# The edge-attribute load of a fused two-layer graph kernel in nine pieces, spread over the item

## The reference

```python
h = relu(layernorm(x));  x = x + attention_layer(h, src, dst)      # 4 heads of 32
h = relu(layernorm(x));  x = x + edge_layer(h, src, dst, edge_attr_128)

# attention_layer
e = leaky_relu(a_s[src] + a_d[dst]);  m = segment_max(e, dst);  e = exp(e - m[dst])
out = segment_sum(e / segment_sum(e, dst)[dst] * xp[src], dst) + bias;  return relu(out)

# edge_layer
edge_agg = segment_sum(edge_attr @ We + be, dst)
x_comb = concat([x, edge_agg]);  h = x_comb + segment_sum(x_comb[src], dst)
return relu(h @ W1 + b1) @ W2 + b2
```

## Time and profile before

| | |
|---|---|
| median of 3 runs | 4222.09 us (4209.79 to 4226.62) |
| profiled execution | 4203.44 us |
| its span | 4200.3 us |
| PE busy | 2634.0 us (63%) |
| DVE busy | 1797.7 us (43%) |
| POOL busy | 1652.3 us (39%) |
| ACT busy | 1001.7 us (24%) |
| DMA, mean over the span | 150 GB/s |

### The profile page before, as it was taken

How to read it: one execution, slowest core, us unless ns; L and a number is a source line. 1 busy time by engine, 2 the same in 40 slices (tenths; PEclk the granted TensorE clock), 3 DMA queues, 4 the chain that set the end, 5 groups by cost and what they waited for, 6 DMA issues and landing times.

```text
span 4200.3 us, 62157 instructions
## 1 busy us (share of the span) xinstructions
PE 2634.0 (63%) x16749; PEld 2099.8 (50%) x16749; DVE 1797.7 (43%) x6117; ACT 1001.7 (24%) x2335; POOL 1652.3 (39%) x1625
## 2 busy tenths in 40 slices
PE   3455555555555555565555555555555559999999
PEld 2343444444444444444344444444444448888887
DVE  6444454445454444444445444444444541111111
ACT  2223223222222222222222222232222230000000
POOL 4544544454444444544455444544454410000000
PEclk7667676667666676666777776667666779999999
DMA  9444444444443444444444444444444446666665
GB/s 183 113 133 123 141 145 143 126 127 143 145 138 116 141 136 130 133 142 137 124 137 145 144 136 124 140 140 136 123 141 144 135 157 221 215 213 221 215 213 180
DMA packets 309819, 630.10 MB, mean 150 GB/s; under 512 B 115675, under 2 KB 239191, under 8 KB 276133
## 3 DMA queue, kind: packets, MB, share of 16 engines
q1 hardware_dynamic: 259679, 514.22, 36.1%
q0 software_dynamic: 50112, 115.56, 13.2%
HBM read 446.35 MB, written 183.24 MB: 150 GB/s over the span
## 4 chain that ended last, share of the span: by engine, by line
PE 42%; another core or an unknown queue 23%; issue 16%; DVE 9%; ACT 5%; SPq 3%; DMA 1%; DVEq 0%; ACTq 0%
PE pv L1184 11%; PE pv L1122 10%; PE pv L1056 8%; PE pt L1184 5%; ACT xsb L809 5%; PE pt L1066 3%; DVE big L1667 2%; PE pa L1066 1%; DVE lks L1650 1%; DVE tabb L1400 1%; PE pa L1110 1%; PE pm L1098 1%; DVE lin L1654 1%; DVE lin L1659 0%
## 5 line engine op out<-in xcount | busy, mean ns | idle before, releaser
L776 POOL DMA_INDIRECT big<-table,idx x1566 | 1615.6, 1032 | 1698.4 <-PE pv L1122 1220.0
L809 ACT ACTIVATE xsb<-pt 128x343 bf16<-128x343 f32 x1044 | 531.5, 543 | 1987.3 <-PE pt L1066 1029.0
L1066 PE MATMUL pt<-tabb 128*128 128x343 bf16 x1044 | 395.4, 381 | 819.9 <-ACT xsb L809 461.6
L1066 PEld LDWEIGHTS pt<-tabb 128*128 128x128 bf16 x1044 | 105.4, 101 | 1053.4 <-ACT xsb L809 577.5
L1056 PE MATMUL pv<-big 128*128 128x128 f32 x3132 | 629.4, 386 | 0.0
L1056 PEld LDWEIGHTS pv<-big 128*128 128x128 f32 x3132 | 613.0, 299 | 1.5
L1122 PE MATMUL pv<-big 128*128 128x133 f32 x3132 | 498.6, 326 | 162.3 <-DVE big L1667 162.3
L1122 PEld LDWEIGHTS pv<-big 128*128 128x128 f32 x3132 | 470.9, 234 | 182.9 <-DVE big L1667 175.5
L1184 PE MATMUL pv<-big,xsb 128*126 128x384 bf16 x2842 | 493.8, 327 | 19.0 <-DVE big L1695 19.0
L1184 PEld LDWEIGHTS pv<-big,xsb 128*126 128x126 bf16 x2842 | 382.8, 136 | 88.2 <-issue 19.0
L1400 DVE TENSOR_TENSOR tabb<-iotah,keyp 128x2064 bf16<-128x2064 bf16 x261 | 320.3, 1227 | 1.4 <-issue 1.1
(11 more groups left out here) (271 smaller groups left out, 2584.0 us busy)
## 6 DMA issues: line engine op xcount, KB each, us to landing
adj<-xsb SPq DMA_DIRECT2D x87, 1543.5 KB
big<-in_edge_attr_dram SPq DMA_DIRECT2D x87, 1152.0 KB, 5.2
xsb<-adj SPq DMA_DIRECT2D x58, 1543.5 KB, 6.7
selb<-rel SPq DMA_DIRECT2D x87, 576.0 KB
tabb<-adj SPq DMA_DIRECT2D x29, 1543.5 KB, 6.7
big<-table,idx POOLq DMA_INDIRECT x1566
state<-sums SPq DMA_DIRECT2D x87, 130.5 KB
sums<-state SPq DMA_DIRECT2D x87, 130.5 KB
```

Source lines behind the costliest of these rows:

```text
L776: pool.indirect_dma_start(out=V[b][:, j, 0:rows], out_offset=None, in_=table, in_offset=bass.IndirectOffsetOnAxis(ap=index[b][:, j:j + 1], ...
L809: return nc.scalar.activation(out_, in_, func, **kw).then_inc(s(name), 1)
L1066: nc.tensor.matmul(pab[c % 3], ohl[:, c, :], ohk[:, c, 0:KW], start=True, stop=True)\
```

## The change

The attributes are loaded in nine transfers of two j each (128 partitions by 256 float32) in place of one of 18 j. Item n of SP now loads those of item n+1, into the other buffer, not of item n+2. Piece 0 waits for `am_b` of item n-1, and pieces 1 to 8 wait for `g_step`, a semaphore that GpSimd raises ahead of every second gather: piece i goes out when gather 2i of item n+1 is about to be issued. Pieces 0 to 3 stand ahead of `store_peak`, pieces 4 to 8 behind the index load. The adjacency store stays one transfer (APIECES = 1), but its place in SP's order is now right behind piece 0.

```diff
-            def load_edges(n, b, it, start):
+            def load_index(b, it, start):
                 after_dma(sp, s(f"gat{b}"), it * J)
                 sp.sem_inc(s("sp_turn"), 1)
                 sp.dma_start(idx[b][:, :], src[bass.DynSlice(start, GE)].rearrange("(p j) -> p j", j=J))\
                     .then_inc(s(f"idx{b}"), 16)
-                after(sp, s("am_b"), n, 2)
-                sp.dma_start(AT[b], attr[bass.DynSlice(start, GE), :].rearrange("(p j) c -> p j c", j=J))\
+
+            def load_attr(b, start, i):
+                js = slice(i * PJ, (i + 1) * PJ)
+                sp.dma_start(AT[b][:, js, :], attr[bass.DynSlice(start, GE), :].rearrange("(p j) c -> p j c", j=J)[:, js, :])\
                     .then_inc(s(f"attr{b}"), 16)
...
+                def spread(lo, hi):
+
+                    for i in range(lo, hi):
+                        if not last:
+                            if i > 0:
+                                sp.wait_ge(s("g_step"), n * PIECES + (PIECES + i))
+                            elif not before_first:
+                                after(sp, s("am_b"), n, 1)
+                            load_attr(1 - b, following, i)
+                        if not before_first and i * APIECES % PIECES == 0:
+                            store_adjacency(n - 1, 1 - b, i * APIECES // PIECES)
+                spread(0, PIECES // 2)
                 store_peak(n, b, base)
-                if not isinstance(n, int) or n + 2 < NG - 1:
-                    load_edges(n + 2, b, it + 1, (n + 2) * GE)
-                elif n + 2 == NG - 1:
-                    load_edges(n + 2, b, it + 1, LAST)
+                if not isinstance(n, int) or n + 2 < NG:
+                    load_index(b, it + 1, LAST if isinstance(n, int) and n + 2 == NG - 1 else (n + 2) * GE)
+                spread(PIECES // 2, PIECES)
...
                 if not (isinstance(n, int) and n < 2):
                     store_projected(n - 2, base_of(n - 2))
-                if not before_first:
-                    store_adjacency(n - 1, 1 - b)
...
                 for j in range(J):
                     if n is not None and j % QUART == 0 and not (isinstance(n, int) and n < 2):
 
                         pool.wait_ge(s("vm_b"), n * QN + (j // QUART + 1 - 2 * QN))
-                        pool.sem_inc(s("g_started"), 1)
+                    if j % PJ == 0:
+                        pool.sem_inc(s("g_step"), 1)
...
-                pe.wait_ge(s(f"attr{b}"), it * 16 + 16)
+                pe.wait_ge(s(f"attr{b}"), (it * 16 + 16) * PIECES)
```

More of the change, by code:

```diff
@@ L57 @@
 FIN = 18
+PIECES = 9
+PJ = J // PIECES
+APIECES = 1
 MAGIC = 0x5f3759df
@@ L72 @@
 FARHI = 1 << 20
-assert COLS <= 128 and OFF <= 256 and NB * 128 <= NPAD and GE == J * 128
+assert J % PIECES == 0 and NB * COLS % APIECES == 0 and COLS <= 128 and OFF <= 256 and NB * 128 <= NPAD and GE == J * 128
 YCH = ((0, 13), (13, 25), (25, 37), (37, 49))
@@ L447, in _ @@
             for b in range(2):
-                load_edges(b, b, 0, b * GE)
+                load_index(b, 0, b * GE)
+            for i in range(PIECES):
+                load_attr(0, 0, i)
             for lo, hi in ((0, SPLIT), (SPLIT, NP)):
@@ L506, in store_projected, with store_adjacency @@
                 sp.dma_start(sums1[bass.DynSlice(base, WIN), :], fy[:, :]).then_inc(s("y_out"), 16)
[L508 to L510 removed]
+            def store_adjacency(n, b, i):
+                if i == 0:
+                    sp.wait_ge(s("ab_ev"), n * J + J)
+                cs = slice(i * (NB * COLS // APIECES), (i + 1) * (NB * COLS // APIECES))
+                sp.dma_start(adj[bass.DynSlice(n, 1), :, cs].rearrange("a p c -> (a p) c"), adjw[b].bitcast(BF16)[:, cs])\
                     .then_inc(s("adj_out"), 16)
@@ L533, in item @@
                     store_sums(n - 1, base_before)
+                last = isinstance(n, int) and n == NG - 1
+                following = 0 if last else LAST if isinstance(n, int) and n == NG - 2 else (n + 1) * GE
+                def spread(lo, hi):
[9 more added lines that the diff above has]
+                spread(0, PIECES // 2)
                 store_peak(n, b, base)
-                if not isinstance(n, int) or n + 2 < NG - 1:
-                    load_edges(n + 2, b, it + 1, (n + 2) * GE)
-                elif n + 2 == NG - 1:
-                    load_edges(n + 2, b, it + 1, LAST)
+                if not isinstance(n, int) or n + 2 < NG:
+                    load_index(b, it + 1, LAST if isinstance(n, int) and n + 2 == NG - 1 else (n + 2) * GE)
+                spread(PIECES // 2, PIECES)
                 if before_first:
@@ L560, in _ @@
             store_residual(NG - 1, base)
-            store_adjacency(NG - 1, 0)
+            for i in range(APIECES):
+                store_adjacency(NG - 1, 0, i)
             store_projected(NG - 1, base)
@@ L624, in extra_item @@
             def extra_item(n, b, it):
-                load_edges(n, b, it, extra(sp, 2, n, LAST))
+                start = extra(sp, 2, n, LAST)
+                load_index(b, it, start)
+                after(sp, s("am_b"), n, 2)
+                for i in range(PIECES):
+                    load_attr(b, start, i)
                 base = extra(sp, 1, n, N)
```

12 lines of the change are left out of this document (6 added, 6 removed).

## The result

The changed kernel took 4261.03 us (median of 4 runs, 4254.14 to 4273.44), the kernel before 4215.94 us (4 runs, three of them the ones that were known before the prediction): a ratio of 1.010, 95% interval 1.0065 to 1.0134. It was 45 us slower where no change was forecast. On which chip each of the two was timed is not on record, and from chip to chip the kernel before alone went from 4169 to 4197 us in later calls, so that part of this 1% can be the chip's.

What follows compares the result with a forecast made beforehand. The prediction took a per-item round of gather issue, late maxima and a chain to the next gathers, 38.1 us, to bound the first loop. Its terms summed to 0, leaving 4203 us profiled; forecast 4216 us, range 4070 to 4330.

Steps and rivals of the forecast that it cites:

- The sum over the ring: Total effect of the change on one item's round: 0 + 0 + 0 us, profiled execution staying at 4203 us.
- the ring: One item's round in the first loop: gather issue, late maxima, then weights and products releasing the next gathers; 38.1 us.
- the 2.5 us from the last gather to the maxima: Stretch after the last gather is issued until TensorE's late maxima are free for VectorE; 2.5 us, expected unchanged.
- the chain of 10 to 13 us: From the maxima through VectorE, TensorE and the weights to the products releasing the next gathers; 10 to 13 us.
- The slower rival: Moved transfers disturb TensorE's exchange of small results or slow gathers: 34 to 100 us, 560 if all items; chance 0.29.
- the one at 1411.96: Existing item with late exchange, 44.78 us, 6.7 over the mean; also cited for its first gather of 0.94 us.
- a longer way from the last gather to the maxima: Gathers landing later beside the store make the 2.5 us behind the last grow; 1 us each item is 84 us.
- the cover of pieces 4 to 8: Their issue on SP, 2.6 to 3.3 us, ends 1.5 us before the load of the sums, costing nothing.
- the first gather no faster: At the gathers' start, the first two stay at 1.5 and 1.3 us; a possible 80 us gain counted as nothing.
- the issue times of pieces 1 to 3: On SP behind the adjacency store, their gathers issued by +8.6 us; some 20 us of room, costing nothing.
- the DMA share of the first 9.65 us: DMA engines' share at the start of the gathers, 0.84 before, expected near 0.5 after the change.
- The rival "much faster": Other-queue traffic among the gathers makes TensorE's results prompt: 27 us an item, 924 us less, to 3300; chance 0.06.

Runs made afterwards that it cites:

- the first measurement: The changed kernel against the kernel before, 4 runs each, before any follow-up: medians 4261.03 and 4215.94 us, ratio 1.010; chips not on record.
- the first two calls: Follow-up sets, each on one chip: both kernels with the adjacency store moved or the attribute load cut, packed or placed differently; 1.0011 to 1.0523 of the kernel before.
- the store put back: The changed kernel with the adjacency store back at the item's end, nine pieces still spread: 1.0186 of the kernel before, later 1.0013 on a chip without late results.
- the cut by partitions: The changed kernel with its nine spread pieces cut into 15 partitions each instead of by j: 1.0157 of the kernel before, later 1.0032 on a chip without late results.
- six doubled products: Adjacency products of blocks 6 to 11 each made twice: in the changed kernel 0.9859, later 1.0002; in the kernel before 0.9851; all against the unmodified kernel before.
- a nudge: The kernel before with a tiny GpSimd memset ahead of gather 16 of every item, meant to delay the last two gathers: 1.0005 of the kernel before.

## Why the prediction was wrong, and where it was right

**The step that failed** is "The sum over the ring: 0 + 0 + 0 us an item. The profiled execution would stay at 4203 us." It prices what the change does to SP and the DMA queues and holds the two other parts of the ring, the 2.5 us from the last gather to the maxima and the chain of 10 to 13 us, as they were, without a reason. Neither stayed. In the mean the first grew by 0.51 us and the chain by 0.28, with 0.18 back from the gathers, 0.62 us an item. The chain is where it shows in the late items: it takes 10.3 us or 13 us according to whether the clock rises 3 us behind TensorE's restart or later, and restarts only 0.2 us apart lie on either side. In the first measurement 24 of 28 late items fell on the wrong side, where 5 of 21 had before. The rows to see it in were there: three items in a row of 37.06, 38.67 and 36.88 us, with a chain of 10.6 us in the first, where the text gives 10 to 13, and a PEclk of 0.82, 0.75 and 0.50 in the windows, that is, means over stretches at 1.2 and 2.4 GHz. I read them as a stable cycle and did not ask what kept it there.

**The slower rival** had the sign and half of the mechanism. It expected more items like the one at 1411.96; these went from 5 to 1. Its other half, a longer way from the last gather to the maxima, was there with 0.5 us where 1 us was priced, partly because the items in which the maxima came out early, as in the earlier trace rows, got fewer (7 with maxima before the last gather was issued, then 1). What it did not have is the clock.

**Right**: the cover of pieces 4 to 8 (2.65 us, ended before the load of the sums was due), no wait of TensorE for attributes, `am_b` no longer waited for, the first gather no faster (1.52 us before, 1.72 after, in the median), nothing from the signals of GpSimd. So the adjacency store, which no longer stands ahead of the gathers, wasn't what slowed them. That it is VectorE fits the trace of the kernel before: of the 238 gathers over 1.1 us 209 ran beside its writing of selection matrices (line 1400), of the 1328 others 81. The item at 1411.96 that the prediction leans on is one of these 81, for VectorE wrote such a matrix from 1412.00 on, beside its gather of 0.94 us; taken alone it would speak against VectorE as well. **Mis-sized**: the issue times of pieces 1 to 3, +7.7 to +10.7 us in the median where +8.6 at the latest was expected, later in single items; and the DMA share of the first 9.65 us, 0.65 for "near 0.5". No effect of either on the ring was seen.

**The rival "much faster"**, results that come promptly, exists as a state: 3388 us, close to the 3300 worked out. But what brings it is not this change nor any kernel here; both kernels are in it on two chips and out of it on the others. Its cause was wrong and its price right by luck: the sum let the gathers' issue bound the ring and took the chain at 10.6 us, 27 us in all; on those chips the chain is 12.7 us, 68 of 82 are long, and the gathers wait some 4.7 us an item for it (401.6 us, 85 times), 28.7 us in all.

**What stays open.** Why TensorE's results wait for the end of the gathers on some chips and not on others, and why in the late items TensorE also starts its own products 2 us apart; for most of these waits no row shows a releaser. And what in the change pushed the first chip's cycle over the cliff: of the variants on the first two calls' chips those with traffic of small or many transfers before or among the gathers were 1.3 to 1.9% slower (the nine of 15 partitions 5.2%), the one transfer issued early 0.8%, the nine behind the index load 0.4%, but the changed kernel was not run beside them there, and of these only the store put back and the cut by partitions were run on a chip without late results, where they are within 0.3%. That the pieces cost 1% is therefore not shown, and that they cost next to nothing (0.1%) is shown only where the results are prompt. Nor is it shown what sets the sign on a given chip: there is no trace of the kernel before from the chips with 0.993 and 1.005.

## What to carry to other kernels

Where a loop is a ring with idle stretches on TensorE, the granted clock is a term of the sum: look at it at the point where TensorE starts again, and allow for a step of some us (here 2.7 in 38) when anything shifts by tenths. A change of 1% in such a kernel says little about the change until it is measured on several chips, and the sign can turn. Work that keeps TensorE busy where it would only wait can be worth as much as the transfers one moves: six doubled products took 0.5% off the changed kernel on both chips where the two ran side by side, and 1.5% off the kernel before on the one where it was tried. A variant is best set against the kernel it was made from, on the same chip: against the kernel before, the same doubled products look like 1.4% on one chip and like nothing on the other. And a nudge must be seen in the trace to have shifted something before its time says anything.

## What the runs showed of the hardware

The kernel before took 4169 to 4216 us on some chips and 3388 us on others; the changed kernel's traces from either kind have the same 65308 instructions, the same 630.17 MB and the usual gather of 0.94 us. On the slower ones the maxima were read 2.3 to 3.2 us behind the last gather's issue (means of the four traces of the two kernels); on the faster ones 1.7 us after the products had begun. And one load cut into nine parts of 15 partitions each cost 5.2%, where nine parts of all 128 partitions cost 1.3% on another chip.
